# Layer 2 attention: order of the score products, of the folds and of the row sums, and block sums of pairs 4 and 5 on VectorE

## The chip, the cores and the metric

The kernel runs on one core of a Trainium2 chip. The metric is the device time of one execution in microseconds (us), lower is better; the time before is the median of three runs. Engines are named as in the profile: PE is TensorE (PEld its weight loads), DVE is VectorE, ACT is ScalarE, POOL is GpSimd, SP is SyncE.

## The reference

Two transformer-like layers over eight batch elements of 512 tokens by 128 features. The change lies in the second layer alone, and there in the causal attention with 16 query heads of 64 features that share one key and one value head. Cut to what matters:

```python
def layer1_attention(x, g1, Wq, Wkv, Wout, g2):
    xn = layernorm(x, g1)                    # per token
    q = (xn @ Wq.T) as 16 heads of 64
    k, v = split(xn @ Wkv.T)                 # 64 features each, shared by all heads
    q, k = l2norm(q * 16) * 4, l2norm(k) * 4
    sim = q @ k.T                            # 512 x 512 for each head
    sim = where(causal_mask, max_neg, sim)
    attn = softmax(sim)
    out = attn @ v                           # 512 x 64 for each head
    return layernorm(concat(out) @ Wout.T, g2)

# second layer: x + layer1_attention(...) + down(silu(gate) * up)
```

## The kernel before

The first layer (its attention, and an expert layer) takes about the first 620 us of the span. Then the second layer handles one batch element after another: a hardware loop over elements 0 to 6 and the last one, element 7, written out after it. The body for one element is `attend(b, last)`, written once for each engine; each engine has its own queue, and the order in the code is the order on the queue. Engines meet at counting semaphores. A `Ring` is a set of PSUM slots with a `full` and a `free` counter.

In `attend` the 16 heads go in 8 pairs, n = 0 to 7, one iteration each. The scores of a pair are computed transposed, keys on partitions, in four key blocks j = 0 to 3 of 128 keys; block j holds queries from 128j on, so 512, 384, 256 and 128 columns for each of the two heads. Queries are split into a high part `q_hi` (rounded by ACT, L1498) and a low part `q_lo` (the difference, made by DVE in `q_low`, L1994); keys likewise (`k_stack`, parts 0 and 1). A score is high*high + high*low + low*high, three products in one accumulation group.

For iteration n the PE queue holds, in this order:

- `scores(n)`: blocks 1 and 3 into ring M, block 2 into ring S, block 0 into ring W. It begins with a wait for `q_lo` of pair n.
- `project_q(n + 2)`, the projection of a later pair; its PSUM bank is free once DVE has scaled pair n + 1 (`q_unit`, L1986).
- `turn_q(n + 1)`, the transposes of the next pair (L500); its bank is free once ACT has taken the exponentials of block 2 of pair n.
- `gate_up(n + 1)` in the first iterations, part of the feed-forward.
- `values1(n - 1)`, attention times values for the pair before, after POOL's masks of it.
- `sums1(m)`, the column sums of the probabilities of pairs 2m and 2m + 1, as products with a matrix of ones that accumulate in the bank `gather`: m = 0 after iteration 5, m = 2 after iteration 6, m = 1 after iteration 7, m = 3 at the end.

ACT takes the exponentials of the three rings (`exp_of`, L1510), squares the projection (L1482), and copies the turned queries into `q_full` and `q_hi` (L1497, L1498). DVE reduces the squares (L1975), makes `q_lo` (L1994), copies the values out (L2031), and runs `q_unit`: L1933, L1935 and L1986. POOL runs `q_length` (L1248, a power of 8 columns), which lies between DVE's reduction and `q_unit`, then the causal masks of the pair (four selects, L1286), and some DMA issues. Squares, reduction, `q_length` and `q_unit` form a chain from one `project_q` to the next.

`fold(n)` (L1269) is a DMA on POOL's queue that adds block 1 of pair n onto block 0 in SBUF, for pairs 0 to 3, so that `sums1(0)` and `sums1(1)` need 12 products instead of 16. It waits for the values of pair n and for the fold before it to have landed. Buffers of probabilities (`probs1`) are six, so pair 6 takes the buffer of pair 0 and waits for `sums1(0)`; pairs 4 and 5 have the buffers `late`.

## Time and profile before

| | us |
|---|---|
| median of 3 runs | 1253.22 |
| lowest, highest | 1252.53, 1253.65 |
| the profiled execution's own time | 1259.26 |
| its span in the profile | 1257.5 |
| start of the ACT copy L1457 that opens elements 2 to 7 | 779.21, 857.88, 936.57, 1015.21, 1093.81, 1172.52 |

So an element of the loop takes 78.6 to 78.7 us, and every one shows the same pattern to within some hundredths. The profiled execution takes 6.0 us more than the median; differences are read within the profile and taken off the median.

How to read the rows below: a timeline row is start, duration, engine, line, operation, what is written and what is read, the number of instructions merged, and in brackets how long the engine was idle before and which work released it. An fp32 product is recorded as two matmuls, so 12 products read as x24 and 16 as x32. The records of neighbouring matmuls overlap by some hundredths, because their ends are modelled.

### The profile page before, as it was taken

The numbers are of one execution on the slowest core, as the hardware profiler recorded it, in microseconds if no ns is written. First come the engines' busy times: TensorE is split into PE (matmuls) and PEld (weight loads), VectorE is DVE, ScalarE is ACT, GpSimd is POOL, SyncE is SP. The second block draws the span as 40 slices with busy tenths as digits, with TensorE's granted clock in tenths as the row PEclk, the third lists the DMA queues.
The fourth block names the chain that finished last, engine by engine and source line by source line (L and its number), as shares of the span: only waits on it lengthen the run. The fifth ranks groups of instructions, "written<-read, shape, count | busy, mean of one in ns | idle before, by whom it ended". The sixth has DMA issues, their size and how long they took to land.

```text
span 1257.5 us, 26722 instructions
## 1 busy us (share of the span) xinstructions
PE 1158.6 (92%) x8667; PEld 789.6 (63%) x8667; DVE 884.8 (70%) x2425; ACT 670.3 (53%) x1290; POOL 484.8 (39%) x691
## 2 busy tenths in 40 slices
PE   5999999999999998898499999999999999999997
PEld 3656656665666654888365757657576575765755
DVE  7888888888888895554475767757677576775744
ACT  2766676667667655454263552635526355263550
POOL 5222212122222312553373572735727357273450
PEclk8999999999999998899699999999999999999998
DMA  3311112120101100222012030120301203012030
GB/s 91 100 47 39 56 26 57 27 70 17 27 17 27 26 10 1 55 58 51 10 23 39 13 54 6 23 38 13 54 4 25 38 13 54 4 25 38 9 52 9
DMA packets 43717, 42.31 MB, mean 34 GB/s; under 512 B 7040, under 2 KB 36224, under 8 KB 43648
## 3 DMA queue, kind: packets, MB, share of 16 engines
q0 software_dynamic: 11008, 17.31, 7.9%
q1 hardware_dynamic: 32640, 24.15, 7.1%
q8 instruction: 34, 0.56, 0.2%
q14 instruction: 35, 0.29, 0.1%
HBM read 13.72 MB, written 6.75 MB: 16 GB/s over the span
## 4 chain that ended last, share of the span: by engine, by line
issue 18%; PE 11%; POOL 7%; DMA 5%; ACT 5%; DVE 5%; POOLq 0%; ACTq 0%; DVEq 0%
DMA arena<-arena 5%; PE gather L496 4%; PE ring_a L496 3%; PE pair L496 3%; ACT arena L1510 3%; POOL arena L1286 3%; POOL arena L1207 2%; POOL q_len L1248 1%; DVE q_parts L1994 1%; POOL late L1286 1%; ACT arena L1490 1%; ACT q_parts L1498 1%; DVE arena L2068 1%; PE ring_d L496 1%; PE pair L500 1%
## 5 line engine op out<-in xcount | busy, mean ns | idle before, releaser
L1353 ACT ACTIVATE arena<-ring_a 128x384 f32<-128x384 f32 (+1 forms) x512 | 253.6, 550 | 148.4 <-PE ring_a L496 148.4
L1102 POOL TENSOR_SCALAR_AFFINE_SELECT arena<-arena 128x512 f32<-128x512 f32 x128 | 82.8, 647 | 367.5 <-ACT arena L1353 367.4
L496 PE MATMUL ring_a<-q_max,rows 128*128 128x384 f32 (+1 forms) x512 | 197.5, 389 | 2.2 <-DVE q_max L1659 1.8
L1645 DVE CUSTOM_DVE_ANT_0 arena<-pair,arena 128x384 bf16<-128x384 f32 (+1 forms) x269 | 161.0, 613 | 23.6 <-PE pair L496 19.2
L1510 ACT ACTIVATE arena<-ring_a 128x1024 f32<-128x1024 f32 x96 | 98.8, 1029 | 105.3 <-PE ring_a L496 105.3
L1248 POOL TENSOR_TENSOR q_len<-q_sum,exponents 128x8 f32<-128x8 f32 x64 | 105.5, 1649 | 111.3 <-DVE q_sum L1975 111.0
L496 PE MATMUL ring_a<-q_parts,k_rows 64*128 64x384 f32 (+2 forms) x1152 | 124.8, 339 | 16.0 <-DVE q_parts L1994 15.2
L496 PE MATMUL ring_a<-arena,v_aug 128*32 128x384 f32 (+1 forms) x1024 | 124.3, 557 | 1.7 <-POOL arena L1102 0.6
L496 PE MATMUL pair<-arena,v_aug 128*64 128x512 f32 (+3 forms) x768 | 114.0, 439 | 4.1 <-ACT arena L1510 3.5
L496 PEld LDWEIGHTS ring_a<-q_parts,k_rows 64*128 64x128 f32 x1152 | 92.2, 186 | 35.0 <-issue 15.8
L496 PE MATMUL pair<-rows,q_rows 128*128 128x384 f32 (+1 forms) x269 | 110.0, 411 | 3.4 <-DMA rows<-k_rows 2.6
L2031 DVE COPY arena<-pair 128x512 f32<-128x512 f32 x64 | 44.2, 690 | 96.6 <-PE pair L496 96.6
L496 PEld LDWEIGHTS ring_a<-q_max,rows 128*128 128x128 f32 x512 | 97.0, 191 | 21.3 <-ACT arena L1353 5.3
L496 PEld LDWEIGHTS pair<-arena,v_aug 128*64 128x64 f32 x768 | 51.1, 136 | 67.4 <-issue 53.6
L1645 DVE CUSTOM_DVE_ANT_0 arena<-gather,arena 128x512 bf16<-128x512 f32 (+1 forms) x124 | 78.0, 629 | 17.6 <-PE gather L496 11.4
L496 PEld LDWEIGHTS pair<-rows,q_rows 128*128 128x128 f32 x269 | 51.3, 191 | 57.5 <-DVE mx L1645 35.5
L1286 POOL TENSOR_SCALAR_AFFINE_SELECT arena<-arena 128x256 f32<-128x256 f32 x192 | 72.0, 403 | 32.2 <-ACT arena L1510 32.1
L1645 DVE CUSTOM_DVE_ANT_0 arena<-ring_d,arena 128x384 bf16<-128x384 f32 (+1 forms) x119 | 73.1, 614 | 9.9 <-PE ring_d L496 6.5
L1975 DVE TENSOR_REDUCE q_sum<-arena 128x8 f32<-128x512 f32 x64 | 43.7, 683 | 49.8 <-ACT arena L1482 49.2
L1994 DVE TENSOR_TENSOR q_parts<-arena,q_parts 128x512 fp32r<-128x512 f32 x64 | 44.3, 692 | 38.0 <-ACT q_parts L1498 35.6
L1415 ACT ACTIVATE arena<-ring_a,arena 128x128 f32<-128x128 f32 x156 | 43.0, 380 | 51.9 <-PE ring_a L496 51.7
L496 PEld LDWEIGHTS gather<-wout_sb,arena 128*128 128x128 f32 x512 | 66.2, 194 | 2.5 <-DVE arena L2068 0.6
(274 smaller groups left out, 2353.5 us busy)
## 6 DMA issues: line engine op xcount, KB each, us to landing
arena<-arena POOLq DMA_DIRECT2D x32, 384.0 KB, 4.4
rows<-k_rows SPq DMA_DIRECT2D x128, 64.0 KB, 2.0
arena<-in_w SPq DMA_DIRECT2D x16, 256.0 KB, 2.8
slots_y<-arena SPq DMA_DIRECT2D x39, 64.0 KB
x_all<-in_x SPq DMA_DIRECT2D x8, 256.0 KB, 4.0
tokens_x<-xn SPq DMA_DIRECT2D x8, 256.0 KB, 2.6
out<-o_t SPq DMA_DIRECT2D x8, 256.0 KB, 2.3
arena<-tokens_x,tokens_now POOLq DMA_INDIRECT x40
```

What stands on the lines that cost most here:

```text
L496: return pe.matmul(out, lhs, rhs, start=start, stop=stop, skip_group_check=True)
L1102: pool.affine_select(out=v, in_=v, compare_op=ALU.is_ge, fill=0.0, base=0, pattern=[[0, HG], [1 if late else -1, P]], channel_multiplier=- ...
L1207: pool.indirect_dma_start(y_back[:, i, :], None, slots_y[0:(TT + NE - 1) * P], bass.IndirectOffsetOnAxis(ap=slots_now[:, i:i + 1], axis=0) ...
L1248: pool.tensor_tensor(q_len[:, half], q_sum[:, half], exponents[:, 2 * NT:4 * NT], ALU.pow).then_inc(s["lens"].sem, s["lens"].add(1))
L1286: ins = pool.affine_select(out=v, in_=v, compare_op=ALU.is_ge, fill=0.0, base=0, pattern=[[0, 2], [1, P]], channel_multiplier=-1)
L1353: act.activation(probs[:, t % NT, h, 0:many], A.slot(("cols", c))[:, 0:many], ACT.Exp).then_inc(A.free.sem, A.free.add(1))
L1415: ins = act.activation(hidden[:, u % 2, c], hidden_bank(u, c), ACT.Relu, bias=staged[:, u, AT_B1 + c:AT_B1 + c + 1])
L1510: act.activation(dst, src, ACT.Exp).then_inc(ring.free.sem, ring.free.add(1))
L1645: dve.tensor_tensor_reduce(dump[:, h % 2, 0:many], M.slot(("max", n))[:, 0:many], masks[:, m, at:at + many], 1.0, LOWEST, ALU.add, ALU.max ...
L1975: dve.reduce_sum(q_sum[:, half_of(s, k)], q_sq, AX.X).then_inc(s["sums"].sem, s["sums"].add(1))
L1994: dve.tensor_tensor(q_lo[:, n % QB, :], q_full, q_hi[:, n % QB, :].bitcast(F32), ALU.subtract).then_inc(s["q_lo"].sem, s["q_lo"].add(1))
L2031: dve.tensor_copy(o1[:, n, :], ring.slot(("o", n))[:]).then_inc(ring.free.sem, ring.free.add(1))
```

## The change

It changes five things in the second layer's `attend`, and nothing elsewhere.

1. In `scores(n)` the products of `q_hi` for blocks 1 and 3 come first, eight of twelve, behind a wait for ACT's copy of `q_hi` in place of the wait for `q_lo`; then the wait for `q_lo`, then the four products with `q_lo`. Blocks 2 and 0 are as before.
2. POOL's `fold(n - 2)` stands at the start of iteration n, ahead of `q_length(n + 1)`; before, `fold(n - 3)` stood at the end of iteration n, after the masks.
3. `sums1(1)` moves from the end of iteration 7 to iteration 6, between `scores(6)` and `turn_q(7)`; `sums1(2)` moves from iteration 6 to the end of iteration 7.
4. DVE adds blocks 1, 2 and 3 of pairs 4 and 5 onto block 0, in three dependent additions each: pair 4 at the start of iteration 6, ahead of `q_low(7)`, and pair 5 after the copy of its values.
5. `sums1(2)` multiplies block 0 alone, 4 products in place of 16, and waits for the six additions.

```diff
@@ scores (TensorE)
-                    pe.wait_ge(s["q_lo"].sem, s["q_lo"].at(b, n + 1))
+                    if n:
+                        pe.wait_ge(S.free.sem, S.emptied(b, ("q.T", n)))
+                    else:
+                        pe.wait_ge(SR["moved"].sem, SR["moved"].at(b, 4))
                     pe.wait_ge(M.free.sem, M.fillable(b, ("probs", n, 0)))
                     sl = M.slot(("probs", n, 0))
-                    side_by_side([sl[:, c * T:c * T + 384] for c in range(2)], 1, n)
-                    side_by_side([sl[:, c * T + 384:c * T + 512] for c in range(2)], 3, n).then_inc(M.full.sem, M.full.add(1))
+                    one, three = [sl[:, c * T:c * T + 384] for c in range(2)], [sl[:, c * T + 384:c * T + 512] for c in range(2)]
+                    part_of(one, 1, n, 0, q_hi, start=True)
+                    part_of(one, 1, n, 1, q_hi)
+                    part_of(three, 3, n, 0, q_hi)
+                    part_of(three, 3, n, 1, q_hi)
+                    pe.wait_ge(s["q_lo"].sem, s["q_lo"].at(b, n + 1))
+                    part_of(one, 1, n, 0, q_lo)
+                    part_of(three, 3, n, 0, q_lo, stop=True).then_inc(M.full.sem, M.full.add(1))
+                    middle_scores(n)
@@ sums1 (TensorE)
-                    for j in (0, 2, 3) if m < N_FOLD // 2 else range(NT):
+                    if m == 2:
+                        pe.wait_ge(s["added4"].sem, s["added4"].at(b, 6))
+                    for j in ((0, 2, 3), (0, 2, 3), (0,), range(NT))[m]:
@@ attend (TensorE)
                     if n + 2 < NP:
                         project_q(n + 2)
+                    if n == 6:
+                        sums1(1)
                     if n + 1 < NP:
                         turn_q(n + 1)
                     if n + 1 < HC:
                         gate_up(n + 1)
                     if n:
                         values1(n - 1)
-                        if n in (5, 6, 7):
-                            sums1((0, 2, 1)[n - 5])
+                    if n == 5:
+                        sums1(0)
+                    if n == 7:
+                        sums1(2)
@@ attend (GpSimd)
                 for n in range(NP):
+                    if 0 <= n - 2 < N_FOLD:
+                        fold(n - 2)
                     if n + 2 < NP:
                         q_length(s, n + 1, b)
...
-                    if 0 <= n - 3 < N_FOLD:
-                        fold(n - 3)
@@ attend (VectorE)
+                def add_blocks(n):
+
+                    dve.wait_ge(O.full.sem, O.filled(b, ("o", n)))
+                    for j in range(1, NT):
+                        dst = probs_of(n, 0)[:, :, j * P:T]
+                        dve.tensor_tensor(dst, dst, probs_of(n, j), ALU.add).then_inc(s["added4"].sem, s["added4"].add(1))
+                        if j < NT - 1:
+                            dve.wait_ge(s["added4"].sem, s["added4"].at(b, s["added4"].n))
+
                 for n in range(NP):
+                    if n == 6:
+                        add_blocks(4)
...
                     if n:
                         values_out(n - 1)
+                    if n == 6:
+                        add_blocks(5)
```

How it moves instructions, first on PE in iterations 6 and 7 (the transposes `pair<-ident,o_n` are `turn_q(7)`; `gather` rows are `sums1`, those that read `late` are `sums1(2)`, and REGISTER_ALU and ISA rows are waits):

```order
 L496 MATMUL ring_a<-q_parts,k_rows 128x512 x6
+L875 REGISTER_ALU
+L496 MATMUL gather<-arena,pick_sum 32x512 x4
+L496 MATMUL gather<-arena,pick_sum 32x256 x4
+L496 MATMUL gather<-arena,pick_sum 32x128 x4
 L812 REGISTER_ALU
 L813 REGISTER_ALU
 L500 MATMUL pair<-ident,o_n 128x128 x4
```

`sums1(1)` now stands between the last score products of iteration 6 and the transposes. Behind the values of iteration 6 the sixteen products of `sums1(2)` are gone. Between the values of pair 6 (iteration 7) and those of pair 7 stands, with the waits of the latter:

```order
-L857 REGISTER_ALU
-L496 MATMUL gather<-arena,pick_sum 32x512 x4
-L496 MATMUL gather<-arena,pick_sum 32x256 x4
-L496 MATMUL gather<-arena,pick_sum 32x128 x4
-L844 REGISTER_ALU
-L847 REGISTER_ALU
+L496 MATMUL gather<-late,pick_sum 32x512 x4
+L862 REGISTER_ALU
+L865 REGISTER_ALU
```

So twelve products become four there, and they are those of `sums1(2)`.

POOL from the DMA issues of iteration 2 to the masks of iteration 3, before:

```order
131 L1207 DMA arena<-slots_y,slots_now 128x128 x2
132 L1246 REGISTER_ALU
133 L1248 TENSOR_TENSOR q_len<-q_sum,exponents 128x8
134 L1278 REGISTER_ALU
135 L1286 AFFINE_SELECT arena<-arena 128x2x128 x2
```

and after:

```order
133 L1231 DMA arena<-slots_y,slots_now 128x128 x2
134 L1289 REGISTER_ALU
135 L1291 ISA
136 L1293 DMA arena<-arena 128x2x384
137 L1270 REGISTER_ALU
138 L1272 TENSOR_TENSOR q_len<-q_sum,exponents 128x8
```

The fold (`DMA arena<-arena`, here `fold(1)`) now stands between the two gathers of iteration 2 and the power of `q_length(4)`. The same holds in iterations 2, 4 and 5; in iteration 5 the row ahead of it is the power of both_roots, the statistics of the next element.

DVE from the end of iteration 5 to the end of iteration 6, before (`xn` and `arena` rows with x4 are the two normalised inputs of the next element):

```order
1593 L1566 TENSOR_SCALAR xn<-x_all,mv,rstd 128x128 x4
1594 L2037 REGISTER_ALU
1595 L1994 TENSOR_TENSOR q_parts<-arena,q_parts 128x512
1596 L2030 REGISTER_ALU
1597 L2031 COPY arena<-pair 128x512
1598 L1566 TENSOR_SCALAR arena<-x_all,mv,rstd 128x128 x4
```

and after:

```order
1593 L1591 TENSOR_SCALAR xn<-x_all,mv,rstd 128x128 x4
1594 L2063 TENSOR_TENSOR late<-late 128x2x384
1595 L2063 TENSOR_TENSOR late<-late 128x2x256
1596 L2063 TENSOR_TENSOR late<-late 128x2x128
1597 L2073 REGISTER_ALU
1598 L2019 TENSOR_TENSOR q_parts<-arena,q_parts 128x512
1599 L2055 REGISTER_ALU
1600 L2056 COPY arena<-pair 128x512
1601 L2063 TENSOR_TENSOR late<-late 128x2x384
1602 L2063 TENSOR_TENSOR late<-late 128x2x256
1603 L2063 TENSOR_TENSOR late<-late 128x2x128
1604 L1591 TENSOR_SCALAR arena<-x_all,mv,rstd 128x128 x4
```

Three additions stand ahead of `q_low(7)` (the `q_parts` row) and three between the copy of the values of pair 5 and the second normalised input.

## Rows read from the trace of the kernel before

**Rows 1.** The page: busy time, share of span and instructions of the engines.

```profile
PE 1158.6 (92%) x8667; PEld 789.6 (63%) x8667; DVE 884.8 (70%) x2425; ACT 670.3 (53%) x1290; POOL 484.8 (39%) x691
```

**Rows 2.** Waits of PE in one element: engine, line, releaser: us, times, longest.

```profile
PE ring_a L496 <- DVE q_parts L1994: 2.1, 3, 1.0
PE ring_d L496 <- DVE o_n L1986: 1.0, 1, 1.0
```

**Rows 3.** Timeline of PE, same element, iterations 0 to 4.

```profile
939.14 1.07 PE L496 MATMUL ring_a<-q_parts,k_rows 64*128 64x384 f32 x12 [0.85 <-DVE q_parts L1994]
...
945.01 1.08 PE L496 MATMUL ring_a<-q_parts,k_rows 64*128 64x384 f32 x12 [1.02 <-DVE q_parts L1994]
945.93 0.57 PE L496 MATMUL pair<-q_parts,k_rows 64*128 64x256 f32 x6
...
947.21 1.16 PE L496 MATMUL ring_d<-wq_sb,o_raw 128*128 128x128 f32 x8
...
967.57 1.16 PE L496 MATMUL ring_d<-wq_sb,o_raw 128*128 128x128 f32 x8 [0.97 <-DVE o_n L1986]
```

**Rows 4.** Timeline of ACT, same element, iteration 0.

```profile
940.34 1.03 ACT L1510 ACTIVATE arena<-ring_a 128x1024 f32<-128x1024 f32 x1 [0.41 <-PE ring_a L496]
...
943.59 0.64 ACT L1498 ACTIVATE q_parts<-pair 128x512 fp32r<-128x512 f32 x1
```

**Rows 5.** Timeline of DVE, same element, iterations 0 and 3.

```profile
938.32 0.69 DVE L1994 TENSOR_TENSOR q_parts<-arena,q_parts 128x512 fp32r<-128x512 f32 x1
...
944.27 0.69 DVE L1994 TENSOR_TENSOR q_parts<-arena,q_parts 128x512 fp32r<-128x512 f32 x1 [0.29 <-ACT q_parts L1498]
...
946.46 0.69 DVE L1986 SCALAR_TENSOR_TENSOR q_nat_sb<-ring_d,q_rn 128x512 f32<-128x512 f32 x1
...
965.13 1.33 DVE L1933 TENSOR_SCALAR q_len<-q_len 128x8 f32<-128x8 f32 x1
```

**Rows 6.** Timeline of POOL, same element, iterations 0, 3, 4 and 6.

```profile
944.05 1.64 POOL L1248 TENSOR_TENSOR q_len<-q_sum,exponents 128x8 f32<-128x8 f32 x1 [3.84 <-DVE q_sum L1975]
...
963.30 1.68 POOL L1248 TENSOR_TENSOR q_len<-q_sum,exponents 128x8 f32<-128x8 f32 x1
964.95 1.48 POOL L1286 TENSOR_SCALAR_AFFINE_SELECT arena<-arena 128x256 f32<-128x256 f32 x4
...
975.78 1.67 POOL L1077 TENSOR_TENSOR rstd<-veps,exponents 128x8 f32<-128x8 f32 x1
...
985.47 1.21 POOL L1269 DMA_DIRECT2D arena<-arena  x1 [1.95 <-PE pair L496]
```

**Rows 7.** Timeline of PE, same element, iterations 5 to 7.

```profile
975.25 2.37 PE L496 MATMUL pair<-late,v_aug 128*64 128x512 f32 x16
977.68 1.72 PE L496 MATMUL gather<-arena,pick_sum 128*32 128x512 f32 x24
...
982.09 0.66 PE L500 MATMUL pair<-ident,o_n 128*128 128x128 f32 x4 [0.58 <-ACT arena L1510]
...
984.98 2.36 PE L496 MATMUL gather<-late,pick_sum 128*32 128x512 f32 x32
987.27 1.07 PE L496 MATMUL ring_a<-q_parts,k_rows 64*128 64x384 f32 x12
...
989.95 2.37 PE L496 MATMUL pair<-arena,v_aug 128*64 128x512 f32 x16 [0.50 <-ACT arena L1510]
```

**Rows 8.** The folds (L1269): all 32 of them, issue to landing.

```profile
DMA to landing us min/median/max: 4.3/4.4/5.7
```

**Rows 9.** Timeline of DVE, same element, iterations 3 and 6.

```profile
968.27 0.69 DVE L1945 TENSOR_TENSOR x_all<-x_all,arena 128x512 f32 x1
...
983.98 0.69 DVE L1994 TENSOR_TENSOR q_parts<-arena,q_parts 128x512 fp32r<-128x512 f32 x1 [2.42 <-ACT q_parts L1498]
```

**Rows 10.** PE: `scores(0)` of element 0, and `sums1(0)` of element 7.

```profile
624.03 1.60 PE L496 MATMUL ring_a<-q_parts,k_rows 64*128 64x384 f32 x12
...
1213.72 1.72 PE L496 MATMUL gather<-arena,pick_sum 128*32 128x512 f32 x24 [1.63 <-DMA arena<-arena]
```

More of the change, by code:

```diff
@@ L821, in side_by_side, with part_of, middle_scores @@
                     return ins[-1]
[L823 to L829 removed]
+                def part_of(outs, j, n, k_part, q_part, start=False, stop=False):
+                    return [mm(outs[c], k_stack[of_half(c), k_part, j * P:(j + 1) * P], q_part[of_half(c), n % QB, j * P:T],
+                               start=start, stop=stop) for c in range(2)][-1]
+                def middle_scores(n):
                     pe.wait_ge(S.free.sem, S.fillable(b, ("probs", n, 1)))
@@ L1513, in attend @@
                 for n in range(NP):
-                    for third in range(3):
+                    for third in (0, 1, 2):
                         exp_of(n, third)
@@ L2012, in attend @@
                 O, L, S, W, Z = (s[k] for k in "OLSWZ")
-                for name in ("q_free", "o_free", "l_free", "e_free", "own", "var", "sums", "q_lo", "h1", "g_free", "inverted", "fin"):
+                for name in ("q_free", "o_free", "l_free", "e_free", "own", "var", "sums", "q_lo", "h1", "g_free", "inverted", "fin", "added4"):
                     s[name].restart()
```

11 lines of the change are left out of this document (6 added, 5 removed).

## The prediction

> **What bounds the kernel now.** I first read the busy times [rows 1]: PE is busy 92% of the span, no other engine over 70%. Then I took one element of the second layer's loop, the one from 936.6 us; the others repeat it. Its waits of PE come to 4.2 us of 78.6 [rows 2, 7]: three for `q_lo`, one for `q_unit` (`o_n`), one for the exponentials ahead of `turn_q(7)` and one ahead of `values1(6)`. So PE bounds, and PE work that goes is time that goes. A wait that goes is worth only what the next wait leaves of it. The next wait is that of `project_q(n + 2)` for `q_unit(n + 1)`: in iteration 1 `q_unit(2)` ends at 946.46 + 0.69 = 947.15 and PE starts `project_q(3)` at 947.21 [rows 3, 5], with no idle time in front, only because PE had been held up by `q_lo` before. That chain (project, squares, reduction, `q_length`, `q_unit`) doesn't contain `q_lo`.
>
> All positions below are of the same element. Its gain at a point is what that point has come forward, counted from the element's start.
>
> **High parts first: +0.5.** `scores(0)` starts at 939.14, when `q_lo` (938.32 + 0.69) is there [rows 3, 5]. Under the new order eight of twelve products can start when `q_hi` and DVE's release of the ring are there, just before 938.32, say 938.45. The twelve take 0.92 from start to start (945.01 to 945.93, [rows 3]); by columns, (384 + 128) for each part, eight take 0.6 and four 0.3. So they fill 938.45 to 939.05, and the group ends some 0.6 sooner. ACT was idle 0.41 before its first exponential [rows 4], so ACT comes forward 0.5 at most (its rows overlap by 0.1), and with it all that follows ACT: `q_hi(1)` (943.59 + 0.64), the squares, `q_unit(2)`. `scores(1)` then starts at `q_hi(1)`, about 943.8 instead of 945.01, and its first group ends 1.1 sooner; but `project_q(3)` must wait for `q_unit(2)`, at 946.7: of 1.1 there stays 0.5. The wait of 0.27 at `scores(3)` turns likewise into one for `q_unit(4)`. Of the 2.1 us of [rows 2] I keep 0.5. The bounds are 0 (if ACT gives nothing) and 2.1.
>
> **The fold ahead of `q_length`: -0.15.** At iteration 2 and 4 POOL has over 1.2 us free before the sum arrives, so a fold of 1.2 (as in [rows 6], the row at 985.47) is covered. At iteration 3 it isn't: POOL starts the power at 963.30 without idle time [rows 6], behind the gathers. With the gain of 0.5, the fold occupies 962.8 to 964.05 and the power starts at 964.05. From the start of a power to the next `project_q`, where DVE waits for POOL, it is 947.21 - 944.05 = 3.16 [rows 3, 6], so `project_q(6)` starts at 967.2 instead of 967.57: the gain falls from 0.5 to 0.35. It falls so little because the 8-column L1933 takes 1.33 there, having begun 0.18 behind the first mask [rows 5, 6]; when DVE waits for POOL itself, as it will, the op starts together with the masks and is short, as it is within the 3.16 of iteration 0. If it takes 1.33 nevertheless, 1.0 more is lost. At iteration 5 the fold delays `q_length(6)` by 1.25, which delays `q_unit(7)` to about 981.4. `turn_q(7)` waits for that, and comes at 983.2 (below): it costs nothing, and without `sums1(1)` as cover it would cost nothing up to 982.09.
>
> **`sums1(0)`: +0.1.** The values before it start at 975.25 and take 2.3 to the next start; it starts at 977.68 instead of 977.55 [rows 7], waiting for `fold(1)`. That fold will have been there for 9 us. The gain stands at 0.48. In the last element that wait is 1.63 [rows 10].
>
> **`sums1(1)` ahead of `turn_q(7)`: +0.64 - 0.56.** PE ends `scores(6)` at 982.09 - 0.58 = 981.51 [rows 7], now at 981.0. Before, it idles here. Now `sums1(1)` fills that, but needs `fold(3)`. POOL can issue it after both_roots' power, 975.78 + 1.67 = 977.45 [rows 6], less 0.35: 977.1; folds land after 4.4 [rows 8], at 981.5. The order of the folds doesn't hold it: `fold(1)` goes at 962.8 and has landed by 968.5 at the latest (5.7, the slowest of [rows 8]), `fold(2)` by 974.2. So a new wait of about 0.5 replaces the old 0.58. Then 1.65 of products (24 records in 1.72), and `turn_q(7)` goes at 983.2, 1.1 later than before. Behind `turn_q(7)` is queued `values1(5)`, and ACT's `q_hi(7)` hangs on it: L1994 ran at 983.98 [rows 9], 1.9 after the transposes, now at 985.1 to 985.8; `scores(7)` starts at 986.0 (next step), so neither part is late.
>
> **`sums1(2)` with 4 products: +1.4.** Sixteen take 2.29 from 984.98 to 987.27 [rows 7], for 4 x (512 + 384 + 256 + 128) columns; the four of 512 are 2048 of 5120 columns, 0.92. They leave iteration 6, so `scores(7)` starts at 983.2 + 0.55 + 2.3 = 986.0 (987.27 before, +1.24), the 0.50 before `values1(6)` stays, since it is `exp` of pair 7 from the same start, and in iteration 7 0.92 stands for 1.65. The gain at `values1(7)` is 1.24 + 0.7 = 1.95.
>
> **DVE's additions: 0.** The nearest row is an addition of 512 columns in SBUF, 0.69 [rows 9]. The three have 768, 512 and 256: about 0.95, 0.69, 0.42 and two waits for the result before, 2.4 a pair. Pair 4 goes into the 2.42 that DVE waits ahead of `q_low(7)` [rows 9], from 982.45 (`q_unit(7)` and the first normalisation are later by the fold) to 984.85; ACT's copy comes at 985.05. Pair 5 runs from 986.8 to 989.2, and `sums1(2)` asks at 991.0. Bounds: nothing, up to the price in the first rival below.
>
> **The wait inside the group: 0.** One more wait for each of 64 `scores`. PE passes such a wait between the M and S groups with starts 0.92 apart and no idle time [rows 3]; the most a row allows is the 0.06 from release to start in iteration 1, 64 x 0.06 = 3.8.
>
> **Sum.** 0.5 - 0.15 + 0.1 + 0.08 + 1.4 = 1.93 for each of elements 1 to 6. Element 0 has no idle time before `scores(0)` [rows 10], so 0.45 less, 1.48. Element 7 is without gathers and both_roots, so the folds go early: 0.5 + 1.63 + 0.64 + 1.4 = 4.2. Together 1.48 + 6 x 1.93 + 4.2 = 17.2. The profiled execution would go from 1259.3 to 1242.0; off the median, **1253.2 - 17.2 = 1236.0**.
>
> **Rivals.**
> *The additions take twice as long (slower).* DVE beside POOL's masks can be held: an op of 8 columns took 1.33 [rows 5]. If a pair's additions take a us, `q_low(7)` is late once 982.45 + a + 0.69 exceeds 986.6, a > 3.5, and `sums1(2)` asks in vain from 983.85 + 2a > 991.0. The gain of an element is used up at a = 4.6; at a = 5, each loop element loses 0.9 and the kernel takes about 1258. Against it stands [rows 9]. Chance 4% for that, 4% for a near 4.6 and about no change.
> *The port is held for a mask at a time.* DVE's additions and POOL's four masks of pairs 6 and 7 (1.5 us a pair, [rows 6]) exclude each other: 2.4 + 1.5 = 3.9 per pair, `q_low(7)` late by 0.4, in all 7 x 0.4 = 3, 1239. Chance 8%. Against it: L1994, which has two SBUF inputs too, ran from 944.27 to 944.96 beside POOL's power of 944.05 to 945.69 and took the same 0.69 as at 938.32 [rows 5, 6]; nothing held it.
> The Trainium skill (SBUF — State Buffer, section SBUF: two separate sides) states that a DVE op with two SBUF inputs and a GpSimd op that reads SBUF lock each other out for the whole instruction. By that rule the additions would be held, as in this rival; the 0.69 beside the power speaks against it, while an addition beside the masks is in no row here.
> *L1933 stays at 1.33 in iteration 3.* 1.0 lost in seven elements: 1243. Chance 10%.
> *`fold(3)` lands after 5.7 instead of 4.4* [rows 8], seven times 1.3: 1245. Chance 8%.
> *Nothing of the new losses comes:* no wait for `fold(3)` and all of `q_lo`'s return up to the next chain, 5 us more: 1231. Chance 9%.
> *The new wait costs 0.06 each:* 1240. Chance 3%.
>
> **How the numbers follow.** The forecast of 1236 holds 54%, with its own range 1233 to 1239. The range 1232 to 1244 takes in the port, L1933 and the wait; outside lie the additions (8%), most of the late landing and half of the better case, under 20% together. Within 0.2% (2.5 us) is about what a measurement can tell from no change: faster 92%, same 4%, slower 4%.
>
> **What would show it.** In the profile after: the waits for `q_lo` in iterations 0, 1 and 3 gone or below 0.1 each and in their place waits of about 0.5 for `q_unit` at `project_q(3)` and `project_q(5)`; L1933 of iteration 3 well under its 1.33; about 0.5 of wait for a DMA before `sums1(1)`, and none before `turn_q(7)`; the additions of a pair within 2.6; the period of an element 76.7 instead of 78.6, and PE busy about 1.4 less in each of eight. The prediction is wrong if the period falls by under 1 or over 3 us; a wait of PE for `added4` or for `q_lo(7)` would show the additions at fault, a longer one at `project_q(6)` the fold.

## The result, and the profile after

| | before | after |
|---|---|---|
| median of the runs timed together, us | 1253.13 (1252.53 to 1253.65, 4 runs) | 1240.12 (1239.02 to 1240.74, 4 runs) |
| profiled execution, its own time and its span, us | 1259.26, 1257.5 | 1239.02, 1237.2 |
| first `gate_up` of layer 2 in that execution, us | 622.03 | 616.38 |
| layer 2, from there to the last instruction, us | 635.5 | 620.8 |

The ratio is 0.9873, with an interval of 0.9844 to 0.9902: 13.0 us, 1.0%, less. The forecast was 17.2 us less, 1236.0, with a range of 1232 to 1244.

The two profiled executions lie 20.3 us apart, more than the medians. Of that, 622.03 - 616.38 = 5.65 lie in the first layer, whose code is the same in both kernels. What the change did is read from layer 2 alone, element by element, each from one first `gate_up` to the next:

| element | 0 | 1 to 6, mean | 7 | together |
|---|---|---|---|---|
| before, us | 79.11 | 78.65 | 84.47 | 635.5 |
| after, us | 79.19 | 76.98 | 79.73 | 620.8 |
| gain: forecast / found | 1.48 / -0.08 | 1.93 / 1.67 | 4.2 / 4.74 | 17.2 / 14.65 |

The first part of the page of after (columns as in [rows 1]):

```profile
span 1237.2 us, 26393 instructions
...
PE 1145.6 (93%) x8475; PEld 782.4 (63%) x8475; DVE 921.7 (74%) x2473; ACT 672.3 (54%) x1290; POOL 490.6 (40%) x691
```

8667 - 8475 = 192 matmuls went, 8 elements of 24, and DVE has 48 instructions and 37 us more, the additions. PE is still the engine that bounds.

For the element that starts at 926.59 in after (936.57 to 936.6 in before; positions below are counted from its first `gate_up`, 926.59 and 937.11), the busy time of the engines. Columns: stretch, its length, busy us of PE, PEld, DVE, ACT and POOL with the number of instructions, granted clock, share of the DMA engines, GB/s. After:

```profile
926.59:1003.59 77.00, 72.74 (x632) 51.28 (x632) 56.15 (x115) 38.30 (x60) 40.51 (x55) 1.00 0.15 27
```

The same of before, over one period from its start:

```profile
936.60:1015.20 78.60, 73.78 (x658) 51.77 (x657) 51.71 (x109) 38.18 (x60) 39.68 (x55) 1.00 0.15 27
```

The clock granted is full in both. Of 1.60 us, 73.78 - 72.74 = 1.04 is PE work, and only 0.56 is idle time of PE, though the waits for `q_lo` alone had been 2.1. The waits of PE in the element of after (answers to [rows 2]) show where the rest stayed:

```profile
PE ring_d L496 <- DVE o_n L2011: 1.5, 1, 1.5
PE ring_d L496 <- DVE q_nat_sb L2011: 0.9, 2, 0.5
PE gather L496 <- DMA arena<-arena: 0.6, 1, 0.6
PE pair L496 <- ACT arena L1535: 0.4, 1, 0.4
PE ring_a L496 <- ACT q_parts L1523: 0.3, 1, 0.3
```

L2011 writes `q_unit` (L1986 before). Those waits were 1.0 and are now 2.4. The wait of 0.6 for a DMA is that for `fold(3)`. The same in PE's order of time (answers to [rows 3] and [rows 7]):

```profile
936.18 1.16 PE L496 MATMUL ring_d<-wq_sb,o_raw 128*128 128x128 f32 x8 [0.55 <-DVE q_nat_sb L2011]
...
949.44 1.16 PE L496 MATMUL ring_d<-wq_sb,o_raw 128*128 128x128 f32 x8 [0.33 <-DVE q_nat_sb L2011]
...
956.96 1.16 PE L496 MATMUL ring_d<-wq_sb,o_raw 128*128 128x128 f32 x8 [1.50 <-DVE o_n L2011]
...
966.94 1.72 PE L496 MATMUL gather<-arena,pick_sum 128*32 128x512 f32 x24
...
971.33 1.72 PE L496 MATMUL gather<-arena,pick_sum 128*32 128x512 f32 x24 [0.56 <-DMA arena<-arena]
972.98 0.66 PE L500 MATMUL pair<-ident,o_n 128*128 128x128 f32 x4
...
975.87 1.08 PE L496 MATMUL ring_a<-q_parts,k_rows 64*128 64x384 f32 x12
...
978.55 2.37 PE L496 MATMUL pair<-arena,v_aug 128*64 128x512 f32 x16 [0.43 <-ACT arena L1535]
980.86 1.06 PE L496 MATMUL gather<-late,pick_sum 128*32 128x512 f32 x8
981.85 2.37 PE L496 MATMUL pair<-arena,v_aug 128*64 128x512 f32 x16
```

Position by position: `project_q(3)` is at 9.59 after and 10.10 before, a gain of 0.51. `project_q(6)` is at 30.37 and 30.46: of the gain 0.09 is left, where 0.35 had been forecast. `scores(7)` is at 49.28 and 50.16, 0.88; `values1(7)`, where the period is all but decided, stands at a gain of 1.5. `sums1(2)` takes 981.85 - 980.86 = 0.99 from start to start where it took 2.29 [rows 7].

### The profile page after: what moved, and what is told of

Read it like the earlier page. It is cut to its first block, busy times and chain, and to the rows that moved or that the text cites. A ratio compares the mean times of both kernels' runs of the same rounds, so it can differ in the third digit from the quotient of the medians.

```text
span 1237.2 us, 26393 instructions
## 1 busy us (share of the span) xinstructions
PE 1145.6 (93%) x8475; PEld 782.4 (63%) x8475; DVE 921.7 (74%) x2473; ACT 672.3 (54%) x1290; POOL 490.6 (40%) x691
## 4 chain that ended last, share of the span: by engine, by line
issue 19%; PE 11%; POOL 9%; DVE 7%; DMA 3%; ACT 1%; POOLq 0%; DVEq 0%; ACTq 0%
PE pair L496 4%; POOL q_len L1272 3%; DMA arena<-arena 3%; PE gather L496 2%; PE ring_d L496 2%; POOL arena L1231 2%; POOL arena L1313 2%; PE ring_a L496 1%; PE pair L500 1%; DVE q_len L1958 1%; DVE stats L1574 1%; POOL arena L1293 1%; DVE arena L2106 1%; DVE q_rn L1960 1%; ACT arena L1515 1%
## 5 line engine op out<-in xcount | busy, mean ns | idle before, releaser
L1272 POOL TENSOR_TENSOR q_len<-q_sum,exponents 128x8 f32<-128x8 f32 x64 | 113.6, 1775 | 85.1 <-DVE q_sum L2000 85.1
L1535 ACT ACTIVATE arena<-ring_a 128x1024 f32<-128x1024 f32 x96 | 99.1, 1032 | 75.9 <-PE ring_a L496 75.7
L496 PE MATMUL ring_a<-q_parts,k_rows 64*128 64x384 f32 (+2 forms) x1152 | 128.3, 344 | 3.4 <-ACT q_parts L1523 2.4
L1313 POOL TENSOR_SCALAR_AFFINE_SELECT arena<-arena 128x256 f32<-128x256 f32 x192 | 80.9, 531 | 45.5 <-ACT arena L1535 43.9
L496 PE MATMUL ring_d<-wq_sb,o_raw 128*128 128x128 f32 x384 | 55.6, 288 | 18.0 <-DVE o_n L2011 9.9
L496 PEld LDWEIGHTS ring_d<-wq_sb,o_raw 128*128 128x128 f32 x384 | 46.5, 191 | 37.5 <-DVE q_nat_sb L2011 18.3
```

Source lines behind the costliest of these rows:

```text
L496: return pe.matmul(out, lhs, rhs, start=start, stop=stop, skip_group_check=True)
L1272: pool.tensor_tensor(q_len[:, half], q_sum[:, half], exponents[:, 2 * NT:4 * NT], ALU.pow).then_inc(s["lens"].sem, s["lens"].add(1))
L1313: ins = pool.affine_select(out=v, in_=v, compare_op=ALU.is_ge, fill=0.0, base=0, pattern=[[0, 2], [1, P]], channel_multiplier=-1)
L1535: act.activation(dst, src, ACT.Exp).then_inc(ring.free.sem, ring.free.add(1))
```

## The experiments

Each edit is on the kernel before or on the changed one, as said. Ratios are to the kernel before, run on the same chip; its median there was 1254.8 for the four kernels of the first part, 1237.0 for the two that move POOL's queue and the two with only the small op rewritten, and 1254.4 for the rest (the power replaced, both kernels again, the three edits together). So times of different groups are compared by ratio or by lengths of elements, which come from the traces.

### One part at a time

**Part 1 alone: before, with the high parts' products first.** The edit is `part_of`, `middle_scores` and the new `scores` of the diff above, nothing else.

> The kernel before with part 1 alone (products with the high parts first). My theory: the three waits for q_lo (2.1 us an element) come back only as far as the chain project_q, squares, reduction, q_length, q_unit allows. The changed kernel's trace shows 0.5 to 0.6 an element at project_q(5); this stays to the element's end here, since nothing else moves. Element 0 loses 0.6, because its first scores took 0.26 + 0.34 + 0.28 us more from start to start than before. Total about 3 us, 1250. The rival, that a wait that goes is time that goes: 8 x 2.1 = 17 us, 1236. A second rival, that the extra wait inside the group costs all of it: 1253 or above.

Measured: 1251.47 (1244.99 to 1255.10, 10 runs), ratio 0.9965, interval 0.9946 to 0.9983. An element takes 78.0 instead of 78.65, a gain of 0.65. Waits of PE in one element:

```profile
PE ring_d L496 <- DVE o_n L2004: 1.0, 1, 1.0
PE ring_d L496 <- DVE q_nat_sb L2004: 0.9, 2, 0.5
PE pair L500 <- ACT arena L1528: 0.6, 1, 0.6
```

The waits for `q_lo`, 2.1 us, are gone, and 0.9 of new ones for `q_unit` stand in their place, at the two places forecast. With the 2.1 returned in full the element would have been 76.5. In element 6 alone it was 76.69, which is taken up below. Element 0 took 79.11, as in before: the 0.6 that it was expected to lose didn't come.

**Part 2 alone: before, with each fold an iteration sooner.**

```diff
                 for n in range(NP):
+                    if 0 <= n - 2 < N_FOLD:
+                        fold(n - 2)
                     if n + 2 < NP:
                         q_length(s, n + 1, b)
...
-                    if 0 <= n - 3 < N_FOLD:
-                        fold(n - 3)
```

> The kernel before with part 2 alone (fold(n - 2) at the head of POOL's iteration n). My theory after the result: the fold between the gathers and q_length(4) delays project_q(6) by about 0.5 us in each of seven elements, against 0.1 that sums1(0) no longer waits, and element 7 gains 1.6: slower by 1 to 1.5 us, 1254.5. The prediction's sizing (0.15 an element): faster by 1.2, 1252. The wait before project_q(6) should be 1.4 to 1.5 instead of 0.97.

Measured: 1258.60 (1255.89 to 1262.93), ratio 1.0024 (1.0005 to 1.0043). Most elements of the loop take 78.74 to 78.84, only 0.1 more than before's 78.65; in the trace, layer 2 is 1.3 longer, since elements 0 and 1 take 80.00 and 79.40, and the last element gains, 83.24 for 84.47. Waits of PE in one element:

```profile
PE ring_a L496 <- DVE q_parts L1994: 2.1, 3, 1.0
PE ring_d L496 <- DVE o_n L1986: 1.5, 1, 1.5
```

Against [rows 2] only the second line differs: 1.5 for 1.0. The fold ahead of `q_length(4)` costs 0.5 at `project_q(6)`, with or without part 1, where the prediction's working made it 0.15. Of this the element gets most back here: `project_q(7)` is only 0.24 later, since the 8-column op of iteration 4 takes 0.16 in this trace and 0.49 in before's, and `sums1(0)` only 0.11, since it no longer waits.

**The additions taken out of the changed kernel**, `sums1(2)` again with sixteen products:

```diff
-                    if n == 6:
-                        add_blocks(4)
...
-                    if n == 6:
-                        add_blocks(5)
...
-                    if m == 2:
-                        pe.wait_ge(s["added4"].sem, s["added4"].at(b, 6))
...
-((0, 2, 3), (0, 2, 3), (0,), range(NT))[m]
+((0, 2, 3), (0, 2, 3), range(NT), range(NT))[m]
```

> The changed kernel without VectorE's additions; sums1(2) has its 16 products again, at its new place. My theory: only the products count, 2.29 against 0.99 us, 1.3 x 8 = 10.4 us slower than the changed kernel, 1250.5, and the additions were hidden. Rival: the additions hold back DVE, POOL's masks or q_low(7) and cost 0.5 an element or more; then the kernel is slower by 6.4 or less, 1246.5 or below.

Measured: 1255.58 (1246.35 to 1260.85), ratio 1.0006 (0.9989 to 1.0024). The profile has layer 2 at 628.8, 7.9 over that of after, and an element at 78.05 instead of 77.0. PE, two of the sums in one element:

```profile
974.52 1.72 PE L496 MATMUL gather<-arena,pick_sum 128*32 128x512 f32 x24 [0.43 <-DMA arena<-arena]
...
984.05 2.36 PE L496 MATMUL gather<-late,pick_sum 128*32 128x512 f32 x32
```

The products cost 1.30 more, the element only 1.05 more. The difference is not the additions' doing: the 8-column op of iteration 4 takes 0.16 here and 0.49 in most elements of after. Element 5 of after has 0.16 too; it takes 76.70 and waits 0.41 for `fold(3)`, and against it the kernel without additions is 1.35 longer. So the additions cost next to nothing. They are the largest single part: without them, the changed kernel's time can't be told from that of the one before, though its layer 2 is 6.7 shorter in the trace.

**The changed kernel with `sums1(1)` behind `turn_q(7)`:**

```diff
-                    if n == 6:
-                        sums1(1)
                     if n + 1 < NP:
                         turn_q(n + 1)
+                    if n == 6:
+                        sums1(1)
```

> The changed kernel with sums1(1) behind turn_q(7) instead of ahead of it. My theory: ahead of the turn it waits 0.56 for fold(3), which takes the place of the 0.58 of idle time that it was to fill; behind the turn the one wait comes back and the other goes, so seven elements stay within 0.1 each and element 7 loses 0.6: 1240.7. Rival: the place ahead of the turn is worth the 0.58 of all eight elements, 1244.8.

Measured: 1244.17 (1243.11 to 1245.32, 4 runs), ratio 0.9910 (0.9889 to 0.9931). Elements 2, 3, 5 and 6 take 77.04 to 77.19, as in after: the wait for the DMA is gone and the one of 0.6 for the exponentials is back. Filling PE with `sums1(1)` is thus worth about nothing in a loop element while `fold(3)` arrives when it does. Elements 1 and 4 take 78.40 and 79.15, with this row of PE in element 4:

```profile
960.82 1.16 PE L496 MATMUL ring_d<-wq_sb,o_raw 128*128 128x128 f32 x8 [2.10 <-DVE o_n L2011]
```

The wait is 0.6 longer than after's 1.50, since the 8-column op on DVE took 1.08 there instead of 0.49. The other 1.5 us come right behind it, where the granted clock of PE is half for 3.4 us (962.0 to 965.4). Both lie ahead of this edit in the element. Element 1 has the same wait of 2.10 with the clock full throughout; its second loss of 0.7 is a wait of 1.29 instead of 0.59 before `turn_q(7)`, with the 8-column op at 1.09 in iteration 5. In after, `sums1(1)` stands in front of that turn and covers such a delay: element 1 of its second trace (below) has the op at 1.09 there too and takes 76.70. The ratio mixes all this.

### Which queue the missing gain is in

After these, my theory was that the fold ahead of `q_length(4)` and the two gathers ahead of it fill POOL, and that `fold(3)` is late because it is issued behind both_roots. The next two kernels move these alone.

**The changed kernel, gathers of iterations 0, 1, 2 as 1, 2, 1** instead of 0, 2, 2, so that the one in front of the power of iteration 3 is gone:

```diff
-                    if not last and n in (1, 2):
-                        fetch(b + 1, (2 * n - 2, 2 * n - 1))
+                    if not last and n in (0, 1, 2):
+                        fetch(b + 1, ((0,), (1, 2), (3,))[n])
```

> The changed kernel with the four gathers of the next element's rows issued 1, 2 and 1 in iterations 0, 1 and 2 instead of 0, 2 and 2, so that the fold of iteration 3 finds POOL free. My theory: the step that was sized too small is the fold between the gathers and q_length(4), so the wait before project_q(6) falls from 1.5 to 1.0 or less and the element from 77.0 to about 76.4; layer 2 shorter by 4 us, 1236 to 1240 by the run's level. Rival, that the loss is not POOL's queue but the 8-column op beside the masks: the wait stays at 1.5 or spreads.

Measured: 1224.58 (1222.98 to 1229.16), ratio 0.9927 (0.9899 to 0.9954). An element takes 75.9, 1.1 less than in after. Waits of PE:

```profile
PE ring_d L496 <- DVE q_nat_sb L2011: 1.6, 2, 1.0
PE gather L496 <- DMA arena<-arena: 0.5, 1, 0.5
```

The wait of 1.5 at `project_q(6)` is gone; of it, 0.7 has come up at `project_q(5)`. There the 8-column op of iteration 2 takes 1.38 where it takes 0.39 in most elements of after; in the last kernel below, with the same order of gathers and that op at 0.38, the wait at `project_q(5)` is 0.32 and that at `project_q(6)` 0.88. The op also has a share in the 1.1: in iterations 3 and 4 it takes 0.16 and 0.24 in most elements here. In elements 3 and 5 it takes 0.50 and 0.48, as in after, and they take 76.33 and 76.36. So 0.65 of the 1.1 are the queue's and about 0.45 the op's.

**And `fold(3)` ahead of both_roots:** the same, with

```diff
-                    if 0 <= n - 2 < N_FOLD:
+                    if 2 <= n < 5:
                         fold(n - 2)
...
+                    if n == 4:
+                        fold(3)
                     if not last and n == 4:
                         both_roots(b + 1)
```

> The same, and fold(3) issued at the end of iteration 4, ahead of the statistics' power, instead of at the head of iteration 5. Theory: fold(3) has landed when PE comes to sums1(1), so the wait of 0.4 to 0.56 there goes, and the filler becomes worth its 0.58: the element 75.9, another 3.5 us less than the kernel with the gathers alone. Rival, that q_unit(7) or ACT then holds turn_q(7): a new wait there of the same size, no change.

Measured: 1220.25 (1219.87 to 1228.05, 4 runs), ratio 0.9889 (0.9836 to 0.9943). An element takes 75.3, another 0.6 less. Waits of PE:

```profile
PE ring_d L496 <- DVE q_nat_sb L2013: 1.6, 2, 1.0
PE pair L496 <- ACT arena L1537: 0.4, 1, 0.4
```

The DMA's line is gone, and the time with it. The 0.56 that the prediction counted as the price of filling PE was the order on POOL's queue, as it had worked out.

### Is it the chain through the power?

**Part 1 on the kernel before, with a multiplication in place of the power:**

```diff
-                                   ALU.pow)
+                                   ALU.mult)
```

> The kernel before with part 1 alone, and POOL's power of 8 columns (1.64 us) replaced by a multiplication of the same columns; so the queries' lengths are not computed. It shortens the chain from one project_q to the next and nothing else. Theory: the wait for q_lo had turned into waits for that chain (0.54 at project_q(3), 0.33 at project_q(5), 0.98 at project_q(6)); they all go, the element falls from 78.0 to 76.2 or below. Rival: PE waits at the same places for ACT's copies or for PSUM, and the element stays above 77.5.

Measured: 1231.66 (one run). An element takes 75.9 where part 1 alone takes 78.0. Waits of PE:

```profile
PE pair L500 <- ACT arena L1528: 0.6, 1, 0.6
PE pair L496 <- ACT arena L1528: 0.5, 1, 0.5
PE ring_a L496 <- ACT q_parts L1516: 0.3, 1, 0.3
```

No wait for `q_unit` is left. So it is the chain to `q_unit` that takes back what the early high parts give: 2.1 us an element hang on it. They are not all the power's, though. The power's place takes 0.20 here instead of 1.64 to 1.68, but the 8-column op behind it in iteration 3 also takes 0.25 instead of 1.33. Element 6 of the kernel with part 1 alone has the op at 0.26 and the power as it was, and takes 76.69: 1.3 of the 2.1 go with the long op, and 0.8 with the power.

### The small op beside the masks

L1933 of before (L1958 of after) scales 8 columns. It took 1.33 in [rows 5]. I took it for held by POOL's masks because it has one input in SBUF and a scalar form, and expected a form with two SBUF inputs to escape. **The changed kernel, and the one before, with it rewritten** (`eps8` is a tile of the constant, set once):

```diff
-                dve.tensor_scalar(length, length, scale, NORM_EPS, ALU.mult, ALU.max)
+                dve.scalar_tensor_tensor(out=length, in0=length, scalar=scale, in1=eps8[...],
+                                         op0=ALU.mult, op1=ALU.max)
```

> The changed kernel with the 8-column scaling of the lengths (tensor_scalar in fp32, 0.16 to 1.4 us beside POOL's masks) written as scalar_tensor_tensor against a tile of the lower bound, same result. Theory: that form isn't held by the masks, as the additions weren't, so it takes 0.2 everywhere; the wait before project_q(6) falls by 0.3 (0.49 becomes 0.2), elements with 1.1 to 1.4 lose it wholly; layer 2 shorter by 2 us in the profile and the spread of the runs narrower. Rival (the lock also holds ops with two SBUF inputs): it still takes 0.36 to 1.3.

Measured: 1234.68 (1228.96 to 1237.09, 10 runs), ratio 0.9969 (0.9947 to 0.9992); elements 77.05, the same as after's. DVE, iteration 2 of one element:

```profile
943.32 1.42 DVE L1960 SCALAR_TENSOR_TENSOR q_len<-q_len,eps 128x8 f32<-128x8 f32 x1
```

> The kernel before with the same rewriting of the 8-column scaling. Theory: it took 1.33 in iteration 3 and 0.49 in iteration 4 of each loop element; without that the wait of 0.97 before project_q(6) goes and the element falls from 78.65 to about 77.6: layer 2 shorter by 7 us, 1246 to 1248. Rival (the op is held in this form too, or q_length is what counts): no change.

Measured: 1236.54 (1234.04 to 1238.78, 10 runs), ratio 0.9987 (0.9967 to 1.0008); elements 77.2 to 77.3. Here the op took 0.24 to 0.27 in iterations 2 to 4, and the wait of 0.97 ahead of `project_q(6)` was gone.

The same form took 1.42 in one kernel and 0.26 in the other, so my theory of the form falls. The next thought was the op's place against the masks. Two rows of DVE and two of POOL from the run with part 1 alone, the first pair of element 5, the second of element 6:

```profile
1033.58 1.48 POOL L1304 TENSOR_SCALAR_AFFINE_SELECT arena<-arena 128x256 f32<-128x256 f32 x4
...
1111.15 1.48 POOL L1304 TENSOR_SCALAR_AFFINE_SELECT arena<-arena 128x256 f32<-128x256 f32 x4
```

```profile
1033.77 1.32 DVE L1951 TENSOR_SCALAR q_len<-q_len 128x8 f32<-128x8 f32 x1
...
1111.32 0.26 DVE L1951 TENSOR_SCALAR q_len<-q_len 128x8 f32<-128x8 f32 x1
```

In the first pair it took 1.32, in the second 0.26, and element 6 was 1.3 shorter than the others for it. The long one ends at 1035.09, just behind the last of the four masks (1035.06), the short one at 1111.58, just behind the first (1111.15 and a quarter of 1.48). So the op ends with one mask or with all four. Its start against the masks doesn't tell which. In the first pair it starts 0.19 behind the first mask, in the second 0.17, but in element 3 of before it starts 0.17 behind it as well and is long:

```profile
886.31 1.48 POOL L1286 TENSOR_SCALAR_AFFINE_SELECT arena<-arena 128x256 f32<-128x256 f32 x4
...
886.48 1.34 DVE L1933 TENSOR_SCALAR q_len<-q_len 128x8 f32<-128x8 f32 x1
```

What decides between them wasn't tried and stays open.

**How much of the gain depends on this op.** In both traces of before, the op of iteration 3 takes 1.32 to 1.34 in every element from 0 to 6. In before with the op rewritten it takes 0.24 to 0.26, an element 77.26 on average and layer 2 624.6. The changed kernel, with 76.98 and 620.8, is 1.67 an element and 14.7 in all below the first, but only 0.3 an element and 3.8 in all below the second. The change has the shorter op too, since the fold delays POOL, so that DVE waits for the power and starts the op together with the masks; but it pays for it with the fold. Part 2 alone has the op at 0.47 to 0.49 in most elements, and they are no shorter. Where the op is short already, the fold's delay has nothing to set against it, and takes back most of what the other parts give.

No trace of before was taken on the chip where its median was 1237.0. That the rewriting gained nothing there (0.9987) suggests that before's op was short there already. The changed kernel with the op rewritten, whose elements are as long as after's, was 0.3% faster than before on that chip (0.9969), and not 1%. So the 13 us hold against executions of before with the long op. Against the short op some 4 us are left; that is argued from the elements and from this ratio, since the changed kernel itself wasn't timed on that chip.

### The three together, and both kernels again

**Before again:**

> The kernel before, unchanged, with a trace of its own from the same chip as the next two. Two of the eight earlier traces show that the 8-column scaling takes either 0.2 to 0.5 or 1.1 to 1.4 us in iteration 3, by some hundredths in its start against the masks. Theory: layer 2 is 635 us where it takes 1.33 (elements of 78.65) and about 625 where it doesn't (elements of 77.3), and the totals of single runs spread between these. Rival: layer 2 is always 635, and the spread of the totals comes from layer 1 alone.

Measured: 1254.80 (1252.65 to 1260.85, 10 runs), ratio 1.0007 (0.9989 to 1.0026), layer 2 at 635.5, as long as in the first trace; its first layer ends at 616.1 instead of 622.0. So the 5.65 us of the first layer belong to an execution and not to a kernel. The op is long in every element from 0 to 6 again, so the case with elements of 77.3 was not seen in this kernel.

**After again:**

> The changed kernel, unchanged, on the same chip as the one before. Theory: its op in iteration 3 starts behind the power and takes 0.49, seldom 1.1, so its elements are 77.0 in either case: against elements of 78.65 it gains 13 to 14.7 us, against elements of 77.3 only 3 to 5, ratio 0.987 or 0.996. Rival (the gain is the same on any chip): ratio 0.987 to 0.989.

Measured: 1243.67 (1240.04 to 1244.60, 4 runs), ratio 0.9899 (0.9864 to 0.9934), layer 2 at 622.4. Its ordinary elements take 76.70 to 76.83, 0.3 less than the 77.0 expected, with the op of iteration 4 at 0.16 instead of 0.49. One element of eight took 78.97, with 2.11 ahead of `project_q(6)`, where the 8-column op took 1.09. As in the kernel with `sums1(1)` behind the turn, the wait is only 0.6 longer; the rest is the clock, half (1.2 GHz) for 3.4 us from 1037.4. PE behind that wait, columns as in the windows above:

```profile
1036.77:1042.23 5.46, 5.46 (x28) 3.21 (x28) 2.62 (x4) 1.68 (x3) 3.56 (x5) 0.69 0.45 72
```

The same work in element 4 takes 3.83 with the clock full. Whether the gain is 3 to 5 us against elements of 77.3, as expected, was not put to the test, since before's elements were long on this chip.

**The changed kernel with both moves on POOL's queue and the two-input form:**

> The changed kernel with the gathers issued 1, 2 and 1, fold(3) in iteration 4, and the 8-column scaling with two inputs. Theory: elements of 75.3 without the wait for q_unit of 1.0 at project_q(5) growing or shrinking, layer 2 of 610 or a little less, faster than the changed kernel by 8 to 11 us whichever mode that is in.

Measured: 1230.79 (1230.44 to 1235.02, 4 runs), ratio 0.9816 (0.9780 to 0.9853): 12.9 us below the changed kernel timed beside it, and the best ratio of all that compute the same, against a before with the long op. Its layer 2 takes 612.2 where the kernel with the two moves alone had 610.5, and its elements 75.86 for 75.32: here the op of iteration 3 takes 0.73 and there 0.16. So the rewritten op adds nothing.

## Why the prediction was right, and where it was off

**High parts first, forecast +0.5: right.** The gain at `project_q(3)` is 0.51, that at `project_q(5)` 0.62, and the waits forecast there are 0.55 and 0.33. Part 1 alone gave 0.65 an element. With the power taken out and the 8-column op short, the rest came back.

**The fold ahead of `q_length(4)`, forecast -0.15: the term that was mis-sized.** It cost 0.42 against the gain of 0.51 at `project_q(3)`, and 0.53 against the 0.62 at `project_q(5)`. POOL and DVE of after, iteration 3 (answers to [rows 5] and [rows 6]):

```profile
952.20 1.42 POOL L1293 DMA_DIRECT2D arena<-arena  x1
953.04 2.30 POOL L1272 TENSOR_TENSOR q_len<-q_sum,exponents 128x8 f32<-128x8 f32 x1
954.70 2.11 POOL L1313 TENSOR_SCALAR_AFFINE_SELECT arena<-arena 128x256 f32<-128x256 f32 x4
```

```profile
955.37 0.49 DVE L1958 TENSOR_SCALAR q_len<-q_len 128x8 f32<-128x8 f32 x1 [1.29 <-POOL q_len L1272]
```

DVE waits for POOL, as forecast, and the 8-column op takes 0.49 instead of 1.33, so the step went the way it was told. Its size was off twice. The fold began at 25.61 (25.69 forecast) but took 1.42 where 1.25 had been counted. The record of the power overlaps it and ends at 955.34; with its usual 1.67 it began at 953.67, position 27.08 instead of 26.94. And from there to `project_q` it is 956.96 - 953.67 = 3.29 where 3.16 had been taken over from iteration 0, with the 8-column op at 0.36 there. Together 0.27: the difference between 0.35 and 0.09, and that between the forecast 1.93 and the 1.67 of a loop element. Part 2 alone has nearly the same numbers (fold 1.43, op 0.49) without part 1. So the fold takes back 0.4 of the 0.5 that part 1 gives. That is already net of the shorter op: in the one element of part 1 alone whose op was short, `project_q(6)` stands at 28.35 without a wait, and in after at 30.37.

**`sums1(0)`, +0.1: right.** There is no wait ahead of it (966.94), and the gain is 0.22.

**`sums1(1)` in front of `turn_q(7)`, forecast +0.64 - 0.56: right.** The wait is 0.56, `turn_q(7)` has none. The working of `fold(3)` held: issued at 966.79, needed at 971.33, 4.54 later. Turning the order back changed nothing in undisturbed elements; issuing the fold ahead of both_roots gave the 0.6.

**`sums1(2)` with four products, forecast +1.4: right.** It takes 0.99 (0.92 forecast), 1.30 less (1.37 forecast).

**The additions, forecast 0: right.** DVE of after, iteration 6 (answers to [rows 9]):

```profile
971.13 2.06 DVE L1591 TENSOR_SCALAR xn<-x_all,mv,rstd 128x128 f32 x4
973.11 2.13 DVE L2063 TENSOR_TENSOR late<-late 128x768 f32<-128x768 f32 x3
975.16 0.69 DVE L2019 TENSOR_TENSOR q_parts<-arena,q_parts 128x512 fp32r<-128x512 f32 x1
976.59 2.27 DVE L2063 TENSOR_TENSOR late<-late 128x768 f32<-128x768 f32 x3
```

A pair's additions take 2.13 and 2.27 (2.4 forecast). `q_lo(7)` follows at once, and no product waits for either. The rival in which they take twice as long didn't come. That of the port held for a mask at a time had no chance to: the first additions end at 975.24, and POOL's masks nearest to them end at 972.86 and start again at 978.18,

```profile
970.98 1.88 POOL L1313 TENSOR_SCALAR_AFFINE_SELECT arena<-arena 128x256 f32<-128x256 f32 x4
978.18 1.90 POOL L1313 TENSOR_SCALAR_AFFINE_SELECT arena<-arena 128x256 f32<-128x256 f32 x4 [5.32 <-ACT arena L1535]
```

so only the second additions (976.59 to 978.86) meet a mask, for 0.7, and they take 0.14 more than the first. The prediction gave that rival its chance by assuming that they run at the same time. What did stretch beside the masks is the normalisation, 2.06 for four.

The Trainium skill (SBUF — State Buffer, section SBUF: two separate sides) states that a DVE op with two SBUF inputs and a GpSimd op that reads SBUF exclude each other for the whole instruction. The op of 8 columns with two inputs fits it where it takes 0.24 to 0.27 and ends with the first mask; where it takes 1.42 it outlasts more than one instruction of GpSimd, and the form with one input does the same. For the additions no run here tests it, since they hardly meet.

**The wait inside the group, forecast 0: right on the path, though PE is held in it.** PE, `scores(0)` of the loop element of after:

```profile
927.93 1.11 PE L496 MATMUL ring_a<-q_parts,k_rows 64*128 64x384 f32 x12 [0.16 <-DVEq L2032]
...
930.36 1.16 PE L496 MATMUL ring_d<-wq_sb,o_raw 128*128 128x128 f32 x8
```

From its start to `project_q` it takes 2.43, where groups that wait for nothing take 2.1. PE is held inside, and the record counts that as busy. This is why PE's busy time fell by 1.04 and not by the 1.30 of products. The chain over `q_unit` covers it.

**Element 0, forecast +1.48: wrong, it lost 0.08.** PE, its `scores(0)` (before: [rows 10]):

```profile
618.38 1.86 PE L496 MATMUL ring_a<-q_parts,k_rows 64*128 64x384 f32 x12
...
621.88 1.16 PE L496 MATMUL ring_d<-wq_sb,o_raw 128*128 128x128 f32 x8
```

The three groups take 3.50 from start to start; before, the same three took 2.66. This is some 0.84 lost at the start. The wait for `fold(3)` is 0.95 in that element, 0.4 more than in the others, and the fold at `project_q(6)` costs 0.43 here too. The 0.84 goes with the granted clock (the third figure from the end, as a share of full speed); first after, then before:

```profile
618.38:621.88 3.50, 3.50 (x25) 3.04 (x24) 0.00 (x0) 3.02 (x4) 0.00 (x0) 0.56 0.00 0
```

```profile
624.03:626.69 2.66, 2.66 (x26) 2.25 (x25) 0.00 (x0) 2.44 (x4) 0.00 (x0) 0.78 0.00 0
```

PE had waited 1.87 and 1.72 before the `gate_up` ahead of them, and the clock was at half (1.2 GHz) up to 621.5 in after and up to 625.2 in before, so 3.1 and 1.2 us of the groups fall into it. The new code of `scores` isn't the reason. Part 2 alone, with the old code, takes 3.54 for the three with 3.1 us at half clock; part 1 alone, with the new one, 2.74 with 1.4. The second profile of the changed kernel has 3.0 with 2.0, and its element takes 78.26. Whether the change has a part in where the half clock ends is not shown.

**Element 7, forecast +4.2: 4.74.** Of it, about 0.4 lie in the output projection behind the loop, which the change does not touch; in before the clock is at half for 3.4 us there (from 1239.6). In the second profile of after such a stretch stands there too, and the element takes 81.31.

**The sum.** -0.08 + 10.0 + 4.74 = 14.65 in the traces against 17.2: 1.56 are missing in element 0, 1.6 in the six loop elements, and 0.5 came on top. The medians give 13.0. That the medians give 1.7 less than the traces can be such things as the second profile of after shows: an element with the op at 1.09 and half the clock behind it (2.2 us), and half the clock in element 7 (1.6 us). That is argued, and can't be shown from executions that were not profiled.

The range held for a before with the long op in iteration 3, which the prediction took from its rows. It reckoned rightly that this op becomes short behind the fold. What it didn't reckon with is that the op can be short in a kernel without the change, against which an element gains 0.3 instead of 1.67.

Of the rivals, the 8-column op at 1.33 in iteration 3 of after didn't come in the first profile, but 1.08 or 1.09 came in single elements of other runs: it wasn't one case or the other, as the prediction had it, but a mixture.

## What to carry to other kernels

A wait that is taken from the bounding engine gives back only the distance to the next chain that ends at it. Here 2.1 us of waits for the low parts gave 0.65, since the norm's chain over POOL's power and the op behind it ended 1.5 later; write that chain out, from the matmul that feeds it to the one that needs it, before the gain is priced. Before a DMA issue is put in front of a small op on a queue, add up what the queue holds in that iteration: behind two gathers the fold left a wait of 1.5 us, behind one 0.88 or less, and spreading the same gathers differently gave 0.65 to 1.1 us an element, against 1.67 for the whole change.

When two executions are compared, take the part of the program that has not changed first: here it held 5.65 of 20.3 us. Then look for short ops whose duration has two values, and for the granted clock of the stretch: either can be mistaken for an effect of an edit. Here a single op of 8 columns moved an element without the change by 1.4 us, nearly as much as the 1.67 that the change gave.

## What the runs showed of the hardware

- A DVE op of 8 columns beside POOL's masks has two durations, 0.26 and 1.32 to 1.34; it ends with the first mask or with the fourth. Its start doesn't decide: 0.17 behind the first mask it took either. With two SBUF inputs both durations are there too (0.26 and 1.42). It made an element of the same kernel 1.3 us shorter.
- The granted clock fell to half for 3.4 us behind a wait of PE of 2.1 us in two elements (2.11 and 2.10), and the work behind it took 5.46 and 5.47 us instead of 3.83; behind a third wait of 2.10 it stayed full. At the start of layer 2 the same three groups of products took 2.66, 2.74, 3.0, 3.50 and 3.54 us with 1.2, 1.4, 2.0, 3.1 and 3.1 us of them at half clock.
- DVE's additions of 768, 512 and 256 columns in SBUF took 2.13 with no mask beside them and 2.27 with one beside their end.
- The folds of the changed kernel land as those before did ([rows 8]); issue to landing, shortest, median and longest:

```profile
DMA to landing us min/median/max: 4.4/4.6/4.9
```

- The kernel before had medians of 1237.0 on one chip and of 1254.8 and 1254.4 in two other groups of runs, which is more than the whole change is worth. It was not profiled on the first. Only times taken beside each other can be compared, and even their ratio is that of one chip.
